# A two-layer graph kernel on one core: where the last 40 node steps scale their output, and when node types are gathered

## The chip, the cores and the metric

The kernel runs on one core of one Trainium2 chip. The metric is the device time of one execution in microseconds. Times inside an execution are microseconds from the start of its profiled span.

## What is computed

```python
# N = 50000 nodes, D = 256, E = 12500 edges (src, dst), dst sorted
# layer 0: attention over edges, 8 heads of 32
qkv = x @ W_qkv.T + b_qkv
att = einsum('mhd,mhd->mh', Q[dst], K[src]) / sqrt(32)
attention = segment_softmax(att, dst)
x = layernorm(x + segment_sum(attention * V[src], dst) @ W_ff.T + b_ff)
# layer 1: messages from node types
W = (edge_attr @ W_dist + b_dist) * cutoff(edge_weight)
agg = segment_sum(embed_table[node_type][src] * W, dst)
x = layernorm(x + concat(x, agg) @ W_comb + b_comb)
```

Most nodes receive no edge. For such a node the result needs only its own row: z = x + b_ff, a layer norm, one 256x256 product with mixed weights (`w_mix`, the identity included), and a second layer norm. The kernel computes that for all 50000 rows, and then overwrites the rows of nodes that receive edges.

## The kernel before

**Node steps.** 98 steps g = 0 to 97 of 512 rows each (the last has 336), as a tile of 128 partitions with four rows of 256 each. Four slots rotate, q = g % 4. For a step:

- SyncE loads `xin` (512 KB, L464) into its slot once the addition and the transposes of the step four before are done, and stores `on` (L473) when both halves of the output scaling have signalled (`n_od`, `n_oa`, L469 to L475). Its queue is in order: at g it issues load g+4, then store g-3, and then whatever edge or softmax traffic belongs to g.
- GpSimd adds the bias row: `zin` = `xin` + `bff_row` (`z_add`, L696). `zin` has two buffers, so the addition of g+3 waits for the statistics of g+1.
- VectorE takes statistics of `zin` (L1340) and moments (L1349), and the reciprocal `r1` (L1357) of ScalarE's root (L1053).
- TensorE transposes `xin` (L797) into two PSUM banks; ScalarE copies them to `zT` with the bias (`zT_copy`, L1046); TensorE multiplies by `w_mix` in two halves (`z_product`, L818; in steps with an edge block in three parts, L811 to L813).
- VectorE makes `yn` (`y`, L1368) in two halves h of two rows, ScalarE squares it with an accumulated sum (`squares`, L1062) and takes the root (L1067), VectorE the reciprocal `r2` (L1378).
- The output scaling `on` = `yn` * `r2`: ScalarE does rows 0 to 2 (`final`, L1075), VectorE row 3 (`final`, L1386). `split(g)` gives the number of ScalarE's rows: 3, and 2 in the last step.

**Order.** There is no scheduler: every engine runs a loop over g, and the order inside it is written out by hand. In step g VectorE does y(g-1,1), statistics g+2, y(g,0), moments g+2, r1(g+1), r2(g-1), its scaling g-1, and then the softmax piece of that step. ScalarE does root 1 (g+1), squares(g-1) with root 2, the transposed copy g+1, and its scaling g-2. TensorE does z_product(g,0), transposes g+1, z_product(g,1). GpSimd does the addition g+3, then gathers and small masks.

**Edge blocks.** Steps 9 to 57 (`LEAD` = 9, `B` = 49, `AFTER` = 58) each also handle one block of 256 edges: GpSimd gathers rows of x for receivers and sources (L705, L708, four indirect DMAs, two blocks ahead), TensorE transposes them and makes Q, K and V in three parts, VectorE takes the low parts and the scores. GpSimd also gathers the node types of the sources (`type_gather`, L699: 128 values in one indirect DMA; 98 are needed in all): one in each edge step, 25 in steps 58 to 82, and 24 more in steps 66 to 89.

**Softmax.** Steps 58 to 97 have no edge block. VectorE runs the segment softmax at the end of its steps, one piece k = g - 58 a step (`softmax_step`): comparisons (k = 0 to 3), scans over 112x896 (k = 4 with its second input in PSUM; 5, 14 and 15 with both inputs in SBUF), rows and carries through TensorE (k = 6, 8, 10, 17, 19), reciprocals (k = 21 to 24, L1536). TensorE's part waits for VectorE at the start of steps 62, 65, 67, 74 and 76 (`chunk_ends`, `carry_columns`, L898 and L904). ScalarE does the exponential at the end of step 71. In step 91 GpSimd casts the types (L761) after its addition and after all gathers have landed, and TensorE transposes them (`type_transposes`, L910) at the head of its step. In steps 85 to 92 SyncE stores the attention and loads the first edge tiles.

**Last pass.** 49 blocks again: GpSimd weighs the values (`weigh`, L715, a product of 128x512), VectorE runs the segment sums, TensorE the products, and the rows go out by indirect DMA. TensorE's first work here waits for ScalarE's `scaled(0)`, which stands behind ScalarE's last scaling.

Of the kernel before, what the change touches and what calls it, by code (L numbers as in the profile page):

```python
# [31 lines left out]
P = 128  # L32
# [14 lines left out]
def after(eng, sem, count):  # L47

    if count > 0:
        eng.wait_ge(sem, count)  # L50


def build(nc, x, src, dst, attr, weight, ntype, w_qkv, b_qkv, w_ff, b_ff, table, w_dist, b_dist, w_comb, b_comb, out):
# [35 lines left out]
    def sb(name, shape, dt=F32):  # L89
        return ctx.enter_context(nc.sbuf_tensor(name, shape, dt))  # L90
# [68 lines left out]
    sd1 = sb("sd1", [P, SLOTS, ROWS])  # L159
    r1 = sb("r1", [P, SLOTS, ROWS])  # L160
    yn = sb("yn", [P, SLOTS, ROWS * D])
    junk = sb("junk", [P, ROWS, D])
    ss = sb("ss", [P, SLOTS, ROWS])
    sd2 = sb("sd2", [P, SLOTS, ROWS])
# [234 lines left out]
    def inside(g):  # L399

        return 0 <= g < G
# [5 lines left out]
    def half(g, j):  # L407

        return 2 + (2 * g + j // 2) % 3

    def split(g):

        return 2 if g == G - 1 else 3

    def within(b):

# [214 lines left out]
    def _(pool):  # L631
# [56 lines left out]
        def z_add(g):  # L688
# [6 lines left out]
            bb = bff_row[0:np_, :].rearrange("p (a d) -> p a d", a=1).to_broadcast([np_, nj, D])  # L695
            pool.tensor_tensor(z, xx, bb, ALU.add).then_inc(n_z, 1)  # L696

        def type_gather(t):
            pool.indirect_dma_start(ty[:, t, :], None, ntype_rows, bass.IndirectOffsetOnAxis(src_i[:, t:t + 1], 0)).then_inc(n_ty, 16)  # L699

# [27 lines left out]
        for g in range(G):  # L728
            if g == LEAD - 3:
                pool.wait_ge(s_idx, 1)  # L730
                gathers(0)
            if g == LEAD - 2:
                gathers(1)
            if inside(g + 3):
                z_add(g + 3)
            b = g - LEAD
            if within(b) and within(b + 2):
                gathers(b + 2)
            if within(b):
                type_gather(b)  # L740
            if 0 <= g - AFTER < 25:
                type_gather(B + g - AFTER)
            if 8 <= g - AFTER < T - B - 17:
                type_gather(B + 17 + g - AFTER)
            if g == AFTER + 1:
                pool.wait_ge(c_mask, 1)
                pool.tensor_scalar(neg_a[:], same_c[:], FAR, -FAR, ALU.mult, ALU.add).then_inc(c_neg, 1)
            if g == AFTER + 2:
                pool.wait_ge(c_mask, 2)
                pool.tensor_scalar(neg_b[:], next_c[:], FAR, -FAR, ALU.mult, ALU.add).then_inc(c_neg, 1)  # L750
            if g == AFTER + 5:
                pool.wait_ge(c_mask, 3)
                pool.wait_ge(c_step, step["running_maximum"])
                pool.tensor_scalar(neg_a[:], first_c[:], FAR, -FAR, ALU.mult, ALU.add).then_inc(c_neg, 1)
            if g == AFTER + 6:
                pool.wait_ge(c_mask, 4)
                pool.wait_ge(c_step, step["chunk_maximum"])
                pool.tensor_scalar(neg_b[:], last_c[:], FAR, -FAR, ALU.mult, ALU.add).then_inc(c_neg, 1)
            if g == AFTER + 33:
                pool.wait_ge(n_ty, 16 * T)  # L760
                pool.tensor_copy(tyf[:], ty[:, :, 0]).then_inc(n_tf, 1)  # L761
        pool.wait_ge(c_step, step["attention"])
        pool.wait_ge(c_out, 16)
        pool.wait_ge(c_same, 16 * NCH)
# [275 lines left out]
    def _(act):  # L1040
        def zT_copy(g):
            for c in range(DC):
                act.wait_ge(n_tp, 2 * g + c + 1)
                after(act, n_y, 2 * (g - 1))
                to = z_hi if in_parts(g) else zT
                act.activation(to[:, g % 2, c, :], ps[:, c, :], ACT.Identity, bias=bff_col[:, c:c + 1]).then_inc(n_tc, 1)  # L1046
# [5 lines left out]
            after(act, n_r1, g - SLOTS + 1)  # L1052
            act.activation(sd1[0:np_, q, 0:nj], mv[0:np_, q, 0:nj, 1], ACT.Sqrt, bias=eps_col[0:np_, :]).then_inc(n_s1, 1)  # L1053

        def squares(g):
            q = g % SLOTS
            np_, nj = size(g)
            after(act, n_s2, g)
            for j in range(nj):
                if j % 2 == 0:  # L1060
                    act.wait_ge(n_yy, 2 * g + j // 2 + 1)
                last = act.activation(junk[0:np_, j, :], yn[0:np_, q, j * D:(j + 1) * D], ACT.Square,  # L1062
                                      scale=float(D ** -0.5), accum_out=ss[0:np_, q, j:j + 1])
            last.then_inc(n_ss, 1)
            act.wait_ge(n_ss, g + 1)
            after(act, n_r2, g - SLOTS + 1)
            act.activation(sd2[0:np_, q, 0:nj], ss[0:np_, q, 0:nj], ACT.Sqrt, bias=eps_col[0:np_, :]).then_inc(n_s2, 1)  # L1067

# [89 lines left out]
        for g in range(G):  # L1158
            b = g - LEAD
            if inside(g + 1):  # L1160
                std1(g + 1)
            if within(b):
                parts(b)
            if inside(g - 1):
                squares(g - 1)
            if inside(g + 1):
                zT_copy(g + 1)
            if inside(g - 2):
                final(g - 2)
            if g == 5:  # L1170
                act.wait_ge(s_echain, 7)
                act.activation(ct[:, 3, :], ct[:, 2, :], ACT.Sin, bias=half_pi[:], scale=-float(np.pi) / CUTOFF).then_inc(s_sin, 1)
            if g == 6 or g == 7:
                weight_copies(g - 6)
            if g == 3:
                act.wait_ge(s_wready, 2)
                for k in range(DC):
                    act.activation(mix_hi[:, k, :], w_mix[:, k, :], ACT.Copy).then_inc(s_mix, 1)
            if within(b):
                q_copy(b)  # L1180
                v_copy(b)
            if g == AFTER + 13:
                act.wait_ge(c_step, step["difference"])
                act.activation(ex_c[:], run_c[:], ACT.Exp, scale=SCALE).then_inc(c_ex, 1)
            if g == AFTER + 33:
                act.wait_ge(s_tyt, 1)
                act.activation(ty_rows[:], ps[0:T, A, 0:P], ACT.Copy).then_inc(s_tyc, 1)
        squares(G - 1)
        final(G - 2)
        final(G - 1)  # L1190

        act.wait_ge(c_out, 16)
# [20 lines left out]
    def _(dve):  # L1213
# [145 lines left out]
        def y(g, h):  # L1359
            q = g % SLOTS  # L1360
            np_, nj = size(g)
            dve.wait_ge(n_r1, g + 1)
            after(dve, n_ss, g - SLOTS + 1)
            after(dve, n_od, g - SLOTS + 1)
            after(dve, n_oa, g - SLOTS + 1)
            dve.wait_ge(n_y, 2 * g + h + 1)
            for j in range(2 * h, min(2 * h + 2, nj)):
                last = dve.scalar_tensor_tensor(out=yn[0:np_, q, j * D:(j + 1) * D], in0=ps[0:np_, half(g, j), (j % 2) * D:(j % 2 + 1) * D],  # L1368
                                                scalar=r1[0:np_, q, j:j + 1], in1=bc[0:np_, :], op0=ALU.mult, op1=ALU.add)
            last.then_inc(n_yy, 1)  # L1370
# [9 lines left out]
        def final(g):  # L1380
            q = g % SLOTS
            np_, nj = size(g)
            dve.wait_ge(n_r2, g + 1)
            after(dve, n_out[q], 16 * (g // SLOTS))
            for j in range(split(g), nj):
                last = dve.tensor_scalar(on[0:np_, q, j * D:(j + 1) * D], yn[0:np_, q, j * D:(j + 1) * D],  # L1386
                                         r2[0:np_, q, j:j + 1], None, ALU.mult)
            last.then_inc(n_od, 1)

        def receiver_low(n):  # L1390
# [223 lines left out]
        rstd1(0)  # L1614
        for g in range(G):
            b = g - LEAD
            if inside(g - 1):
                y(g - 1, 1)
            if inside(g + 2):
                stats(g + 2)  # L1620
            if within(b):
                receiver_low(b)
            y(g, 0)
            if within(b):
                source_low(b)
            if inside(g + 2):
                moments(g + 2)
            if inside(g + 1):
                rstd1(g + 1)
            if inside(g - 1):  # L1630
                rstd2(g - 1)
            if in_parts(g + 1):
                z_low(g + 1)
            if within(b):
                scores(b)
            if inside(g - 1):
                final(g - 1)
            if g == 4:
                edge_floats()
            if g == 5:  # L1640
                edge_cutoffs()
            if g == 6:
                edge_indices()
            if g == 6 or g == 7:
                weight_low(g - 6)
            if g == 7:
                bias_parts()
            if g == 4:
                dve.wait_ge(s_mix, 2)
                for k in range(DC):  # L1650
                    dve.tensor_tensor(mix_lo[:, k, :], w_mix[:, k, :], mix_hi[:, k, :], ALU.subtract).then_inc(s_mix, 1)
            if g == LEAD + 30:
                table_parts()
            softmax_step(g - AFTER)
        y(G - 1, 1)
        rstd2(G - 1)
        final(G - 1)

        dve.wait_ge(c_out, 16)
        dve.wait_ge(c_same, 16 * NCH)  # L1660
# [38 lines left out]
```

## Time and profile before

| | us |
|---|---|
| median of 3 runs | 1166.85 (1166.7 to 1167.99) |
| the profiled execution's own time | 1165.22 |
| its span | 1163.5 |
| TensorE busy, share of the span | 1072.6, 92% |
| VectorE | 987.6, 85% |
| ScalarE | 799.1, 69% |
| GpSimd | 694.1, 60% |

The profile is of one execution. Busy time is the union of an engine's instructions; on GpSimd the issue of an indirect DMA counts as an instruction. PE is TensorE's multiplication, PEld its weight load, DVE VectorE, ACT ScalarE, POOL GpSimd, SPq SyncE's queue. "[0.55 <-ACT zT L1046]" behind a row says that the engine was idle for 0.55 us before it, and what ended that. PEclk is the granted TensorE clock as a share of 2.4 GHz.

### The profile page before, as it was taken

How to read it: one execution, taken by the hardware profiler on the slowest of the kernel's cores; microseconds unless marked ns; L12 is line 12 of the kernel's file. 1: busy time of each engine (PE TensorE's matmuls, PEld its weight loads, DVE VectorE, ACT ScalarE, POOL GpSimd, SP SyncE). 2: the span in 40 equal slices, each digit the busy share in tenths (PEclk: the TensorE clock that was granted, in tenths of full speed). 3: DMA queues.
4: the chain of work that ended last, by engine and by line, in shares of the span. 5: the costliest groups of instructions: out<-in, count | busy, mean ns of one | idle time of the engine just before them, and what ended most of it. 6: DMA issues, size and time to landing. Idle time of an engine off the chain costs nothing.

```text
span 1163.5 us, 24929 instructions
## 1 busy us (share of the span) xinstructions
PE 1072.6 (92%) x7106; PEld 987.7 (85%) x7106; DVE 987.6 (85%) x2646; ACT 799.1 (69%) x2464; POOL 694.1 (60%) x558
## 2 busy tenths in 40 slices
PE   4959999999999999999887878879999999999994
PEld 3759999999999999999666767668888888888883
DVE  4978888888888888887989899868888888888882
ACT  2857777777777777777778878884555555555553
POOL 4367777777777777775777776413444444444442
PEclk9979999999999999999989999989999999999997
DMA  4856666666666666665545556646666666666740
GB/s 147 274 210 211 229 226 225 229 232 221 220 219 218 218 228 229 224 224 179 199 148 179 181 183 224 235 154 168 174 171 177 182 183 185 187 185 180 185 139 33
DMA packets 121385, 227.23 MB, mean 195 GB/s; under 512 B 33587, under 2 KB 61486, under 8 KB 121184
## 3 DMA queue, kind: packets, MB, share of 16 engines
q1 hardware_dynamic: 104000, 189.54, 49.0%
q0 software_dynamic: 17248, 36.08, 11.4%
q8 instruction: 59, 0.97, 0.4%
q14 instruction: 78, 0.64, 0.2%
HBM read 137.84 MB, written 93.59 MB: 199 GB/s over the span
## 4 chain that ended last, share of the span: by engine, by line
PE 78%; DVE 8%; issue 6%; ACT 3%; DMA 2%; POOL 1%; SPq 1%; DVEq 0%; POOLq 0%; ACTq 0%
PE ps L938 14%; PE ps L920 7%; PE ps L818 5%; PE ps L797 5%; PE ps L812 4%; PE ps L811 4%; PE ps L856 4%; PE ps L855 4%; PE ps L857 4%; PE ps L813 4%; PE ps L969 4%; PE ps L853 2%; DVE stat L1340 2%; DVE yn L1368 2%; PE ps L962 2%
## 5 line engine op out<-in xcount | busy, mean ns | idle before, releaser
L696 POOL TENSOR_TENSOR zin<-xin,bff_row 128x1024 f32<-128x1024 f32 x98 | 233.4, 2384 | 78.6 <-DVE stat L1340 62.7
L818 PE MATMUL ps<-w_mix,zT 128*128 128x256 f32 x780 | 193.5, 396 | 33.8 <-ACT zT L1046 32.7
L818 PEld LDWEIGHTS ps<-w_mix,zT 128*128 128x128 f32 x780 | 146.2, 196 | 62.9 <-ACT zT L1046 41.8
L1368 DVE SCALAR_TENSOR_TENSOR yn<-ps,r,bc 128x256 f32<-128x256 f32 x391 | 169.2, 473 | 28.6 <-PE ps L813 15.3
L1062 ACT ACTIVATE junk<-yn 128x256 f32<-128x256 f32 x391 | 158.1, 416 | 45.6 <-DVE yn L1368 45.3
L715 POOL TENSOR_TENSOR ev<-abc,v 128x512 f32<-128x512 f32 x49 | 66.2, 1353 | 198.1 <-DVE zeT L1560 198.1
L1340 DVE BATCH_NORM_STATS2 stat<-zin 128x6 f32<-128x256 f32 x391 | 136.2, 409 | 9.4 <-POOL zin L696 9.4
L705 POOL DMA_INDIRECT xd<-in_x_dram,idx x98 | 94.2, 961 | 78.3 <-PE ps L841 47.0
L1075 ACT ACTIVATE on<-yn,r 128x256 f32<-128x256 f32 x293 | 126.7, 501 | 0.0
L721 POOL DMA_INDIRECT out_dram<-oe,idx x98 | 98.1, 1001 | 33.8 <-issue 22.1
L811 PE MATMUL ps<-mix_hi,z_hi 128*128 128x256 f32 x392 | 114.8, 293 | 2.6 <-DVE z_lo L1405 2.6
L699 POOL DMA_INDIRECT ty<-in_node_type_dram,src_i x98 | 101.9, 1040 | 24.5 <-issue 20.9
L1386 DVE TENSOR_SCALAR on<-yn,r 128x256 f32<-128x256 f32 x98 | 110.4, 1126 | 1.7
L708 POOL DMA_INDIRECT xs<-in_x_dram,idx x98 | 93.6, 955 | 29.9 <-issue 29.6
L812 PE MATMUL ps<-mix_lo,z_hi 128*128 128x256 f32 x392 | 110.8, 283 | 0.0
L813 PE MATMUL ps<-mix_hi,z_lo 128*128 128x256 f32 x392 | 110.0, 281 | 0.0
L797 PE MATMUL ps<-ident,xin 128*128 128x128 f32 (+1 forms) x782 | 105.9, 280 | 0.0
L797 PEld LDWEIGHTS ps<-ident,xin 128*128 128x128 f32 (+1 forms) x782 | 94.4, 146 | 6.2 <-issue 1.4
L938 PE MATMUL ps<-wc,agg 128*128 128x256 f32 x392 | 98.4, 379 | 0.0
L920 PE MATMUL ps<-num,wff 128*128 128x256 f32 x392 | 93.4, 381 | 0.0
L938 PE MATMUL ps<-w_mix,zeT 128*128 128x256 f32 x392 | 92.6, 379 | 0.0
L1153 ACT ACTIVATE oe<-ye,er 128x256 f32<-128x256 f32 x98 | 44.5, 501 | 61.5 <-DVE er L1609 61.5
(202 smaller groups left out, 3079.4 us busy)
## 6 DMA issues: line engine op xcount, KB each, us to landing
xin<-in_x_dram SPq DMA_DIRECT2D x97, 512.0 KB, 4.7
out_dram<-on SPq DMA_DIRECT2D x97, 512.0 KB, 2.9
xd_o<-xdT SPq DMA_DIRECT2D x49, 256.0 KB
v_o<-vT SPq DMA_DIRECT2D x49, 256.0 KB, 2.0
v<-v_o SPq DMA_DIRECT2D x49, 256.0 KB
abc<-a_o SPq DMA_DIRECT2D x196, 64.0 KB
xd<-xd_o SPq DMA_DIRECT2D x49, 256.0 KB, 4.3
sbc<-same_o SPq DMA_DIRECT2D x49, 128.0 KB, 4.0
```

What stands on the lines that cost most here:

```text
L696: pool.tensor_tensor(z, xx, bb, ALU.add).then_inc(n_z, 1)
L797: last = pe.transpose(ps[:, c, j * P:j * P + np_], xin[0:np_, q, j * D + c * P:j * D + (c + 1) * P], ident[0:np_, 0:np_])
L811: mm(to, hi, mix_hi[:, k, :], start=k == 0, stop=False)
L812: mm(to, hi, mix_lo[:, k, :], start=False, stop=False)
L813: last = mm(to, lo, mix_hi[:, k, :], start=False, stop=k == DC - 1)
L818: last = mm(ps[0:np_, half(g, j), (j % 2) * D:(j % 2 + 1) * D], zT[:, g % 2, k, j * P:j * P + np_], w_mix[:, k, :], start=k == 0, stop=k = ...
L920: last = mm(bank(FF[par])[:, c, :], wff[:, k, c * P:(c + 1) * P], num[:, par, k, :], start=k == 0, stop=k == DC - 1)
L938: last = mm(to[:, t, :], cols_of[:, k, t * P:(t + 1) * P], weights[:, k, :], start=k == 0 and not bias, stop=k == DC - 1)
L1062: last = act.activation(junk[0:np_, j, :], yn[0:np_, q, j * D:(j + 1) * D], ACT.Square, scale=float(D ** -0.5), accum_out=ss[0:np_, q, j:j ...
L1075: last = act.activation(on[0:np_, q, j * D:(j + 1) * D], yn[0:np_, q, j * D:(j + 1) * D], ACT.Copy, scale=r2[0:np_, q, j:j + 1])
L1340: last = dve.bn_stats(stat[0:np_, g % SLOTS, j, :], zin[0:np_, g % 2, j * D:(j + 1) * D])
L1368: last = dve.scalar_tensor_tensor(out=yn[0:np_, q, j * D:(j + 1) * D], in0=ps[0:np_, half(g, j), (j % 2) * D:(j % 2 + 1) * D], scalar=r1[0 ...
```

## The change

`relaxed(g)` is true from step 58 on. Four things differ.

1. **Scaling.** From step 57 on `split` is 2: ScalarE scales rows 0 and 1 of each step, and a new GpSimd `final` scales rows 2 and 3 in one instruction of 128x512, with `r2` repeated along each row. VectorE scales nothing there.
2. **ScalarE's order** in steps 58 to 97: squares of the first half of g-1, scaling g-2, transposed copy g+1, squares of the second half, root 2. `squares` is cut in two, each half with its own wait and signal, so that waits on `n_ss` count two a step. VectorE takes `r2(g-2)` at the head of step g and not `r2(g-1)` behind r1.
3. **Type gathers.** Two in each of the 49 edge steps, none later.
4. **VectorE's scaling** in steps up to 56 also writes the sum of each row to a new tile `row_sum`, which nothing reads.

```diff
+    def relaxed(g):
+        return g >= AFTER
     def split(g):
-        return 2 if g == G - 1 else 3
+        return 2 if relaxed(g + 1) else 3
...
+        def final(g):
+            q = g % SLOTS
+            np_, nj = size(g)
+            n = nj - split(g)
+            pool.wait_ge(n_r2, g + 1)
+            after(pool, n_out[q], 16 * (g // SLOTS))
+            rows = [a[0:np_, q, split(g) * D:nj * D].rearrange("p (j d) -> p j d", j=n) for a in (on, yn)]
+            scale = r2[0:np_, q, split(g):nj].rearrange("p (j a) -> p j a", a=1).to_broadcast([np_, n, D])
+            pool.tensor_tensor(rows[0], rows[1], scale, ALU.mult).then_inc(n_od, 1)
...
             if within(b):
-                type_gather(b)
-            if 0 <= g - AFTER < 25:
-                type_gather(B + g - AFTER)
-            if 8 <= g - AFTER < T - B - 17:
-                type_gather(B + 17 + g - AFTER)
+                type_gather(2 * b)
+                type_gather(2 * b + 1)
+            if relaxed(g - 1):
+                final(g - 2)
...
+        final(G - 2)
+        final(G - 1)
...
-        def squares(g):
+        def squares(g, h):
             after(act, n_s2, g)
-            for j in range(nj):
-                if j % 2 == 0:
-                    act.wait_ge(n_yy, 2 * g + j // 2 + 1)
+            act.wait_ge(n_yy, 2 * g + h + 1)
+            for j in range(2 * h, min(2 * h + 2, nj)):
                 last = act.activation(junk[0:np_, j, :], ...)
             last.then_inc(n_ss, 1)
-            act.wait_ge(n_ss, g + 1)
+        def std2(g):
+            act.wait_ge(n_ss, 2 * (g + 1))
...
             if inside(g - 1):
-                squares(g - 1)
-            if inside(g + 1):
-                zT_copy(g + 1)
-            if inside(g - 2):
+                squares(g - 1, 0)
+            if relaxed(g):
                 final(g - 2)
+                if inside(g + 1):
+                    zT_copy(g + 1)
+                squares(g - 1, 1)
+                std2(g - 1)
+            else:
+                if inside(g - 1):
+                    squares(g - 1, 1)
+                    std2(g - 1)
+                if inside(g + 1):
+                    zT_copy(g + 1)
+                if inside(g - 2):
+                    final(g - 2)
...
-        squares(G - 1)
+        squares(G - 1, 0)
         final(G - 2)
+        squares(G - 1, 1)
+        std2(G - 1)
         final(G - 1)
...
             for j in range(split(g), nj):
                 last = dve.tensor_scalar(on[0:np_, q, j * D:(j + 1) * D], yn[0:np_, q, j * D:(j + 1) * D],
-                                         r2[0:np_, q, j:j + 1], None, ALU.mult)
+                                         r2[0:np_, q, j:j + 1], None, ALU.mult, ALU.add, accum_out=row_sum[0:np_, q, j:j + 1])
...
+            if relaxed(g - 1):
+                rstd2(g - 2)
             if inside(g - 1):
                 y(g - 1, 1)
...
-            if inside(g - 1):
+            if inside(g - 1) and not relaxed(g):
                 rstd2(g - 1)
...
-            if inside(g - 1):
+            if inside(g - 1) and not relaxed(g):
                 final(g - 1)
...
+        rstd2(G - 2)
         y(G - 1, 1)
         rstd2(G - 1)
-        final(G - 1)
```

## Rows read from the trace of the kernel before

**Rows 1.** Windows by stage.

```profile
core 0: us, PE busy (x) PEld busy (x) DVE busy (x) ACT busy (x) POOL busy (x), PEclk, DMA share, GB/s
...
87.00:542.00 455.00, 453.89 (x3847) 450.68 (x3845) 395.85 (x1019) 349.84 (x1005) 340.26 (x284) 1.00 0.67 223
...
551.00:773.00 222.00, 186.41 (x959) 155.88 (x958) 205.39 (x614) 179.23 (x584) 145.24 (x91) 0.96 0.54 185
...
727.00:738.00 11.00, 9.87 (x52) 7.95 (x50) 10.93 (x30) 8.76 (x30) 5.69 (x3) 1.00 0.94 304
```

**Rows 2.** Timeline of a plain step: start us, length us, engine.

```profile
711.17 1.39 DVE L1340 BATCH_NORM_STATS2 stat<-zin 128x6 f32<-128x256 f32 x4
...
712.42 1.25 ACT L1046 ACTIVATE zT<-ps,bff_col 128x512 f32<-128x512 f32 x2
...
712.70 2.37 POOL L696 TENSOR_TENSOR zin<-xin,bff_row 128x1024 f32<-128x1024 f32 x1 [1.28 <-DVE stat L1340]
...
713.72 1.59 PEld L818 LDWEIGHTS ps<-w_mix,zT 128*128 128x128 f32 x8 [0.55 <-ACT zT L1046]
...
713.78 1.44 DVE L1386 TENSOR_SCALAR on<-yn,r 128x256 f32<-128x256 f32 x1
...
715.14 0.86 DVE L1368 SCALAR_TENSOR_TENSOR yn<-ps,r,bc 128x256 f32<-128x256 f32 x2
...
715.34 1.01 PEld L797 LDWEIGHTS ps<-ident,xin 128*128 128x128 f32 x8
...
716.32 1.60 PEld L818 LDWEIGHTS ps<-w_mix,zT 128*128 128x128 f32 x8
...
717.18 1.25 ACT L1046 ACTIVATE zT<-ps,bff_col 128x512 f32<-128x512 f32 x2
```

**Rows 3.** Line groups: VectorE's scaling, 551 to 725 us; ScalarE's scaling, squares.

```profile
L1386 DVE TENSOR_SCALAR on<-yn,r x30: 353/1433/1448, 552.1 to 723.3; 128x256 f32<-128x256 f32 x30
...
L1075 ACT ACTIVATE on<-yn,r 128x256 f32<-128x256 f32 x293 | 126.7, 501 | 0.0
...
L1062 ACT ACTIVATE junk<-yn 128x256 f32<-128x256 f32 x391 | 158.1, 416 | 45.6 <-DVE yn L1368 45.3
```

**Rows 4.** Timeline: transposed copies of the last two steps.

```profile
765.22 1.25 ACT L1046 ACTIVATE zT<-ps,bff_col 128x512 f32<-128x512 f32 x2
...
769.67 1.25 ACT L1046 ACTIVATE zT<-ps,bff_col 128x512 f32<-128x512 f32 x2
```

**Rows 5.** Line groups: GpSimd's type gathers, 97 to 540 us; its L715.

```profile
L699 POOL DMA_INDIRECT ty<-in_node_type_dram,src_i x48: 947/952/966, 100.0 to 534.9; - x48
...
L715 POOL TENSOR_TENSOR ev<-abc,v 128x512 f32<-128x512 f32 x49 | 66.2, 1353 | 198.1 <-DVE zeT L1560 198.1
```

**Rows 6.** Timeline: two scans on VectorE, gathers beside them.

```profile
576.10 2.01 DVE L1489 TENSOR_TENSOR_SCAN run_c<-neg_a,ps 112x896 f32<-112x896 f32 x1
576.16 0.97 POOL L699 DMA_INDIRECT ty<-in_node_type_dram,src_i  x1
...
582.77 2.01 DVE L1493 TENSOR_TENSOR_SCAN seg_c<-neg_b,run_c 112x896 f32<-112x896 f32 x1
582.84 2.75 POOL L699 DMA_INDIRECT ty<-in_node_type_dram,src_i  x1 [0.15 <-issue]
```

**Rows 7.** Timeline: ScalarE's transposed copies around a reciprocal step.

```profile
689.66 1.25 ACT L1046 ACTIVATE zT<-ps,bff_col 128x512 f32<-128x512 f32 x2
...
695.79 1.25 ACT L1046 ACTIVATE zT<-ps,bff_col 128x512 f32<-128x512 f32 x2
```

**Rows 8.** Timeline: TensorE's weight loads, start of step 67.

```profile
602.43 0.46 PEld L904 LDWEIGHTS ps<-one_col,cr 1*112 1x112 f32 x4 [3.33 <-DVE cr L1460]
602.91 3.02 PEld L818 LDWEIGHTS ps<-w_mix,zT 128*128 128x128 f32 x8
```

**Rows 9.** Timeline: the type transposes of step 91.

```profile
739.35 2.35 POOL L696 TENSOR_TENSOR zin<-xin,bff_row 128x1024 f32<-128x1024 f32 x1 [3.46 <-DMA xin<-in_x_dram]
...
742.03 0.32 PE L910 MATMUL ps<-ident,tyf 128*98 128x128 f32 x1 [3.87 <-POOL tyf L761]
```

More of the change, by code:

```diff
@@ L161, in build @@
     yn = sb("yn", [P, SLOTS, ROWS * D])
+    row_sum = sb("row_sum", [P, SLOTS, ROWS])
     junk = sb("junk", [P, ROWS, D])
@@ L1064, in squares @@
             last.then_inc(n_ss, 1)
-            act.wait_ge(n_ss, g + 1)
+        def std2(g):
+            q = g % SLOTS
+            np_, nj = size(g)
+            act.wait_ge(n_ss, 2 * (g + 1))
             after(act, n_r2, g - SLOTS + 1)
@@ L1362, in y @@
             dve.wait_ge(n_r1, g + 1)
-            after(dve, n_ss, g - SLOTS + 1)
+            after(dve, n_ss, 2 * (g - SLOTS + 1))
             after(dve, n_od, g - SLOTS + 1)
```

## The prediction

> **What bounds the kernel now.** I read the busy shares and the stages first, then the timeline of one plain step, then what ends each wait. In the 49 steps with an edge block TensorE is busy 453.9 of 455 us, so nothing else counts there; the last 40 node steps take 222 us, or 5.55 us a step, with TensorE at 186 us, ScalarE at 179 us and VectorE at 205 us [rows 1]. A plain step of this stretch (no softmax work) shows why. From one transposed copy on ScalarE to the next are 717.18 - 712.42 = 4.76 us. VectorE starts its output scaling at 713.78 and its next instruction at 715.14, 0.07 us after GpSimd's addition (712.70 + 2.37) ended; TensorE waited 0.55 us for a transposed copy [rows 2]. The scaling has a median of 1433 ns but a shortest of 353 ns [rows 3]: some 1.1 us of it is waiting until GpSimd is through. So VectorE bounds the plain step, and a fifth to a quarter of its step is a wait for the other engine. Softmax steps are longer, as their extra instruction comes behind it.
>
> **The other floors.** TensorE: 8 + 8 + 8 weight loads start at 713.72, 715.34 and 716.32, the last lot runs 1.60 us, so 4.2 us a step [rows 2]. ScalarE: at the very end VectorE waits for others, and copy to copy is 769.67 - 765.22 = 4.45 us [rows 4]; one output row less, 501 ns by its record [rows 3] and some 0.4 of the engine's time where records overlap, makes 4.0 to 4.05. VectorE without the scaling: 4.76 - 1.36 = 3.4 us. GpSimd: 2.37 us of addition, and the new scaling of 128x512 with two inputs. The nearest row is the product at L715, 1.35 us [rows 5]; bounds are 1.2 us (half of the 1024-wide addition) and, if the repeated scalar operand costs double, 2.7 us. I take 1.35, the same shape and engine: 2.37 + 1.35 + 0.25 of gaps = 4.0 us. The plain step should so become 4.25 us, TensorE's.
>
> **What the shared path of GpSimd and VectorE does.** Two neighbours in the trace separate it. A 2.01 us scan whose second input is in PSUM runs beside a type gather of 0.97 us; a scan of the same 2.01 us with both inputs in SBUF stretches the gather that starts 0.07 us behind it to 2.75 us [rows 6]. So GpSimd and a two-input VectorE instruction exclude each other, and the VectorE scaling (one input) is excluded too when it comes second [rows 2, 3]. No row shows a two-input VectorE instruction coming second, since the scaling has always taken up the wait ahead of it. Its cost is bounded by nothing and by the 1.36 us the scaling now waits; I take 1.36, as the scaling behaves so. The Trainium skill, SBUF — State Buffer, "Who interferes with whom", says that a VectorE instruction with two SBUF inputs contends with a GpSimd one that reads SBUF, and that whichever starts first blocks the other fully; by it the sum is the one below, without it that of the first rival.
>
> **The sum, part by part** (profiled execution, 1165.2 us; the median of the three is 1166.85, 1.6 above).
> 1. Scaling leaves VectorE, steps 58 to 97. GpSimd's addition still starts right behind the statistics, so whatever VectorE issues after its reciprocals still meets it.
>  - Six steps end in softmax work with one SBUF input or none shared (62: scan on PSUM, 70, and 79 to 82, four reciprocals, in steps of 695.79 - 689.66 = 6.13 us [rows 7]). Each gains 1.36 less 0.08 for the reciprocal now at the head: 7.7 us.
>  - Six plain steps (71, 84 to 87, 92) go from 4.76 to 4.25: 3.0 us.
>  - Steps 88 and 89 took 11 us together, with 304 GB/s and DMA at 0.94 [rows 1], because the rows of x and so the addition came late and the scaling waited for it; 93 is like them. The scaling's wait is gone, and the statistics that need the addition come a step later: 3.4 us.
>  - In 64, 66 and 75 copies out of PSUM run ahead of the blocked instruction: 1.6 us.
>  - Thirteen steps (58 to 61, 63, 65, 68, 69, 72, 73, 77, 78, 83) end in an instruction with two inputs or a fast copy or scalar form. It waits for the addition in the scaling's place. Gain nothing; the reciprocal at the head costs 0.08 each: -1.0 us.
> 2. ScalarE's order. In plain steps both orders fit under 4.25. Where TensorE has waited for VectorE (602.43, waited 3.33 us [rows 8]; likewise in 74 and 76), the step is a chain: products, transposes, copy, and now two squares and the root behind the copy before VectorE's next step may start. Two squares more, 0.42 each with some 0.1 of reading the accumulator [rows 3], less one output row (0.4): -0.5 each, -1.5 us. Scaling on ScalarE now stands ahead of the copy and waits for the reciprocal at the head of VectorE's step; in a 6 us step this delays TensorE inside its slack, at nothing. Without that slack it would cost what VectorE is late by, up to 1.4 us a step.
> 3. Clock. After the wait at 602.43 eight loads took 3.02 us and not 1.60 [rows 8], and the granted clock shows the lower level there. The like wait ahead of step 76 was a little shorter and grows by about half a us, so I charge half of such a stretch (half of 1.4 to 1.7): -0.8 us.
> 4. The type transposes in step 91. TensorE waited 3.87 us for GpSimd's cast, which stood behind an addition whose rows were 3.46 us late [rows 9]. Now 1.35 us of scaling stands between addition and cast, and at a faster pace the rows are later against the step: I take 2 us, between none and 5. -3.4 us.
> 5. End. Step 94 was VectorE catching up and now costs TensorE's 4.25; the last squares stand behind the copy: -1.0 us. The last GpSimd scaling and the first L715 product (1.35 each) lie beside ScalarE's last rows and the first edge matmuls.
> 6. Type gathers, edge stage. GpSimd is idle 455 - 340.3 = 114.7 us there, 2.34 a block [rows 1]; one more gather is 0.95 us plus 0.3 of issue [rows 5], hidden by that idle time, and no row gather, addition or SP queue entry behind it is needed sooner than a block later. Its 128 tiny transfers add little to DMA. Nothing in, nothing out: 0. In the tail, its removal frees GpSimd for the scaling. If the cover were gone each would cost 1.25.
> 7. The accumulating scaling, steps 0 to 56. It should no longer wait for GpSimd, nor be as short as 0.35; hidden by TensorE in the edge stage. In steps 0 to 8 it may give or take 1 us: 0.
> 8. SP: a store now waits for GpSimd too, whose scaling of a step ends over two steps before the load behind that store is wanted: 0, or 1 us a step should GpSimd fall behind.
>
> Gains 15.7, costs 7.7: net 8.0 us, 1157.2 in the profiled execution, **1158.5** at the median. Own range: 1154 to 1163.
>
> **Rivals.** A measurement tells 0.2% (2.3 us) from no change.
> - **No blocking when VectorE is second.** Then the thirteen steps gain too: 13 x 1.15, less 1 for the score transposes in 59: 14 us more, **1145**. For it: no row shows such a block. Against: the stretched gather [rows 6] and the scaling [rows 3]. 18%.
> - **The tail gives it back.** The rows of x come 5 us late for the type handshake and not 2, and three more waits of TensorE bring the low clock at 1.5 to 1.7 us each: 8 us, **1166**. For: both have happened once [rows 8, 9]. Against: less waiting elsewhere keeps TensorE busier. 10%.
> - **GpSimd becomes the bound (slower).** Place: its scaling in each of 40 steps. If the repeated scalar makes it 2.7 us, its step is 5.3 us; 14 plain steps (71, 84 to 96) lose 0.95 each and the rest about 1: +14, **1173**. It decides from about 2.3 us. Against: L715 [rows 5]. For: no row has this operand form. 7%.
> - **The second gather stretches in the edge stage.** If it took 2.75 us [rows 6] with 0.3 of issue, 0.7 us a block would stick out: 49 x 0.7 = 35, **1193**. It decides when more than 2.34 us is added a block. Against: 48 of 48 gathers there take 947 to 966 ns. 5%.
> - My forecast: 60%.
>
> **Numbers.** Faster by over 0.2% (below 1164.5): 60 + 18 + 2 of the second rival = 80%; within it 8%; slower 7 + 5 = 12%. The range takes in the first rival and my own bounds and stops short of the slower ones: 1145 to 1165.
>
> **What would show it.** Right: plain steps at 4.2 to 4.3 us with no VectorE scaling; reciprocal steps near 4.8; in step 63 the scan starts when the addition ends, and its step is no shorter than before; the edge stage still saturated by TensorE; scaling there near 0.5 us; GpSimd's scaling 1.3 to 1.4 us; TensorE waiting 5 us or more for the cast in step 91. Wrong: softmax steps shorter by 1.3 us (first rival), a plain step above 4.5, GpSimd busy nine tenths and more of the tail, or a longer edge stage.

## The result and the profile after

The changed kernel takes 1178.06 us, median of seven runs, against 1166.77 for the kernel before in the same session: a ratio of 1.0097, 95% interval 1.0077 to 1.0116. The prediction was 1158.5 us with a range of 1145 to 1165. The profiled execution took 1179.73 us (span 1178.0), and its trace is compared here with that of before. Windows by stage of the changed kernel:

```profile
core 0: us, PE busy (x) PEld busy (x) DVE busy (x) ACT busy (x) POOL busy (x), PEclk, DMA share, GB/s
87.00:560.00 473.00, 449.91 (x3764) 440.71 (x3764) 388.59 (x1041) 343.25 (x987) 392.01 (x327) 1.00 0.62 210
578.00:786.00 208.00, 187.71 (x959) 160.01 (x959) 174.37 (x576) 165.94 (x550) 128.41 (x80) 0.93 0.61 200
```

Beside [rows 1] two things stand out. TensorE, which had been busy 453.9 of 455 us in the edge-block steps, is now idle 23 of 473 us there. And GpSimd, taken as busy, has gone from 340 to 392 us. The last 40 steps are shorter. Measured from the first VectorE instruction of a step's y to that of another step (by this measure "the edge stage" is steps 9 to 57 and "the last steps" are 58 to 96, in all that follows):

```
                        before    after
steps 0 to 8             60.77    59.06
steps 9 to 57           463.90   492.23   (edge blocks: 9.44 -> 10.10 us each from step 13 on)
steps 58 to 96          222.33   208.08
```

So the gain that the forecast was about is there, and larger (14.3 us). A loss of 28.3 us stands in a stage for which the forecast said 0.

**What GpSimd does in an edge block.** Timelines of GpSimd, before (a block from 328.50 on) and after (from 303.67 on), start and length in us:

```profile
328.50 2.40 POOL L696 TENSOR_TENSOR zin<-xin,bff_row 128x1024 f32<-128x1024 f32 x1
331.93 0.96 POOL L705 DMA_INDIRECT xd<-in_x_dram,idx  x1 [1.02 <-PE ps L841]
333.19 0.96 POOL L705 DMA_INDIRECT xd<-in_x_dram,idx  x1 [0.30 <-issue]
...
336.97 0.95 POOL L699 DMA_INDIRECT ty<-in_node_type_dram,src_i  x1 [0.30 <-issue]
337.94 2.41 POOL L696 TENSOR_TENSOR zin<-xin,bff_row 128x1024 f32<-128x1024 f32 x1
```

```profile
303.67 2.41 POOL L701 TENSOR_TENSOR zin<-xin,bff_row 128x1024 f32<-128x1024 f32 x1
306.24 1.24 POOL L720 DMA_INDIRECT xd<-in_x_dram,idx  x1 [0.16 <-issue]
307.78 0.95 POOL L720 DMA_INDIRECT xd<-in_x_dram,idx  x1 [0.30 <-issue]
...
311.55 0.95 POOL L714 DMA_INDIRECT ty<-in_node_type_dram,src_i  x1 [0.30 <-issue]
312.81 0.95 POOL L714 DMA_INDIRECT ty<-in_node_type_dram,src_i  x1 [0.30 <-issue]
313.76 2.41 POOL L701 TENSOR_TENSOR zin<-xin,bff_row 128x1024 f32<-128x1024 f32 x1
```

Before, GpSimd waited once in a block for another engine, 1.02 us ahead of the first xd gather (for TensorE's transposes, which free the buffer). Nearly all its other idle time is the 0.30 us "issue" between gathers, which is part of what a gather costs: it stays when nothing else is waited for, as the block after shows. After, it waits for nobody: 313.76 - 303.67 = 10.09 us of its own work, one instruction behind the other, is the block.

**How the other engines are held.** In the changed kernel z_add has slid until it lies on VectorE's xd_lo. First VectorE's row in the same block, then all xd_lo of the kernel (shortest, median, longest in ns), then the group of weight loads at the head of q_product, 124 to 559 us:

```profile
305.29 1.34 DVE L1425 TENSOR_TENSOR xd_lo<-xdT,xd_hi 128x512 fp32r<-128x512 f32 x1
```

```profile
L1425 DVE TENSOR_TENSOR xd_lo<-xdT,xd_hi x49: 670/1342/1493, 84.6 to 568.2; 128x512 fp32r<-128x512 f32 x49
```

```profile
L869 PEld LDWEIGHTS ps<-b_rows,ones_r 128*128 128x128 f32 x172 | 32.3, 188 | 31.3 <-issue 31.3
```

z_add ends at 303.67 + 2.41 = 306.08. xd_lo (two inputs in SBUF) starts at 305.29 and ends 0.55 us after that, so it stood still for most of the 0.79 us that z_add had left: a median of 1342 ns, and 674 before. q_product needs xd_lo, so TensorE stands idle ahead of its loads at L869, 31.3 us over 43 blocks (before, 4.1 us over 44). The profile puts that down to "issue", though what is late is xd_lo; only the order of starts shows it (xd_lo ends at 306.63, the first of these matmuls starts at 306.73). The xd gather that starts beside xd_lo takes 1.24 us, where the others take 0.95.

**The last 40 steps.** The timeline of the scan of step 63 with z_add beside it and of TensorE's weight loads at the type transposes of step 91, then all of GpSimd's and VectorE's scaling:

```profile
604.99 2.37 POOL L701 TENSOR_TENSOR zin<-xin,bff_row 128x1024 f32<-128x1024 f32 x1
...
605.89 3.35 DVE L1524 TENSOR_TENSOR_SCAN seg_c<-neg_b,run_c 112x896 f32<-112x896 f32 x1
...
755.51 0.16 PEld L926 LDWEIGHTS ps<-ident,tyf 128*98 128x98 f32 x1 [5.13 <-POOL tyf L775]
755.58 3.08 PEld L834 LDWEIGHTS ps<-w_mix,zT 128*128 128x128 f32 x8
```

```profile
L711 POOL TENSOR_TENSOR on<-yn,r x41: 682/1040/1050, 581.3 to 789.8; 128x512 f32<-128x512 f32 x40, 112x256 f32<-112x256 f32 x1
...
L1417 DVE TENSOR_SCALAR_CACHE_REDUCE on<-yn,r x57: 469/470/482, 31.0 to 574.2; 128x256 f32<-128x256 f32 x57
```

The scan takes 3.35 us and not 2.01 [rows 6]: it is held until z_add ends (607.36) and ends 1.88 us after that. So a two-input instruction is held when it comes second, as forecast, and the first rival is out. GpSimd's scaling takes 1.04 us. The accumulating scaling takes 0.47 us in all 57 cases. In step 91 TensorE's loads wait 5.13 us for the cast, where they waited 4.27 before, and its next eight loads take 3.08 us, where they took 2.28 before and take 1.60 at the full clock.

### The profile page after: what moved, and what is told of

Read it like the earlier page. It is cut to its first block, busy times and chain, and to the rows that moved or that the text cites. A ratio compares the mean times of both kernels' runs of the same rounds, so it can differ in the third digit from the quotient of the medians.

```text
span 1178.0 us, 25043 instructions
## 1 busy us (share of the span) xinstructions
PE 1080.1 (92%) x7106; PEld 992.1 (84%) x7106; DVE 955.5 (81%) x2662; ACT 784.6 (67%) x2424; POOL 739.4 (63%) x599
## 4 chain that ended last, share of the span: by engine, by line
PE 81%; issue 7%; DVE 5%; ACT 3%; POOL 2%; DMA 1%; DVEq 0%; SPq 0%; POOLq 0%; ACTq 0%
PE ps L954 14%; PE ps L834 8%; PE ps L936 7%; PE ps L813 5%; PE ps L872 4%; PE ps L827 4%; PE ps L871 4%; PE ps L873 4%; PE ps L829 4%; PE ps L828 4%; PE ps L985 4%; PE ps L869 3%; PE ps L978 2%; PE ps L893 2%; PE ps L894 2%
## 5 line engine op out<-in xcount | busy, mean ns | idle before, releaser
L834 PEld LDWEIGHTS ps<-w_mix,zT 128*128 128x128 f32 x780 | 148.9, 199 | 42.5 <-ACT zT L1062 19.5
L720 POOL DMA_INDIRECT xd<-in_x_dram,idx x98 | 106.4, 1086 | 35.0 <-issue 22.3
L1094 ACT ACTIVATE on<-yn,r 128x256 f32<-128x256 f32 (+1 forms) x253 | 111.0, 500 | 16.3 <-DVE r L1409 16.3
L827 PE MATMUL ps<-mix_hi,z_hi 128*128 128x256 f32 x392 | 114.7, 293 | 2.7 <-DVE z_lo L1436 2.7
L723 POOL DMA_INDIRECT xs<-in_x_dram,idx x98 | 93.7, 956 | 29.9 <-issue 29.6
L714 POOL DMA_INDIRECT ty<-in_node_type_dram,src_i x98 | 93.7, 956 | 29.6 <-issue 29.6
L1126 ACT ACTIVATE vT<-ps,bqkv 128x256 f32<-128x256 f32 x98 | 41.1, 471 | 92.3 <-PE ps L895 92.3
```

Of the source, the lines that this page charges most:

```text
L827: mm(to, hi, mix_hi[:, k, :], start=k == 0, stop=False)
L834: last = mm(ps[0:np_, half(g, j), (j % 2) * D:(j % 2 + 1) * D], zT[:, g % 2, k, j * P:j * P + np_], w_mix[:, k, :], start=k == 0, stop=k = ...
L1094: last = act.activation(on[0:np_, q, j * D:(j + 1) * D], yn[0:np_, q, j * D:(j + 1) * D], ACT.Copy, scale=r2[0:np_, q, j:j + 1])
```

## The experiments

Slack is what an engine could take on in a block without making the block longer. Theory G: the loss is the second gather, which is more than GpSimd's real slack of some 1.03 us a block. Theory S: it reaches TensorE through z_add holding up xd_lo. Rivals: some other part of the change lengthens the blocks, or the last steps' gain comes from the gathers having left them. Ratios are to the kernel before, with 95% intervals; stage times are taken as in the table above.

**The gathers alone.** In the kernel before:

```
-                type_gather(b)
-            if 0 <= g - AFTER < 25: ...
-            if 8 <= g - AFTER < T - B - 17: ...
+                type_gather(2 * b)
+                type_gather(2 * b + 1)
```

> The kernel before with one edit: both type gathers in each edge-block step and none in the last 40 steps. Theory G (the second gather fills GpSimd): GpSimd has 1.03 us of real slack in a block and the gather takes 0.95 and 0.30 to issue, so blocks go from 9.44 to about 10.1 us from the third or fourth block on, +25 to +30 us in the edge stage; the last 40 steps as before or up to 2 us shorter (gathers gone), type transposes +3 as they wait for the cast: 1190 to 1197 in all. Rival V (the accumulating scaling or another part of the change slows the blocks): blocks stay at 9.44 and the time within 3 us of the kernel before.

Measured: 1186.64 us, 1.0182 (1.0148 to 1.0215). Steps 9 to 57 take 485.13 us, +21.2, blocks 9.88 us: theory G, though less than the 10.1 and the 25 to 30 us expected. The last steps take 220.7 (-1.6); steps 90 and 91 with the type transposes are 2.7 us shorter (9.81 for 12.55), where 3 us more were expected. Here it is the scaling that is held (all of it, shortest, median and longest in ns; then one in a block's timeline):

```profile
L1383 DVE TENSOR_SCALAR on<-yn,r x98: 344/1664/2545, 30.5 to 795.4; 128x256 f32<-128x256 f32 x97, 112x256 f32<-112x256 f32 x1
```

```profile
310.00 2.15 DVE L1383 TENSOR_SCALAR on<-yn,r 128x256 f32<-128x256 f32 x1
```

xd_lo keeps 0.67 us and no gather is stretched. A block's GpSimd work is then 9.83 to 9.9 us: 2.40, six gathers at 0.95 and their gaps. By the order of starts, VectorE, held up by the scaling, is what passes that on here.

**The change without its gathers.** The edit is the reverse, made in the changed kernel.

> The changed kernel with its type gathers as in the kernel before: one per block, the other 49 in the last 40 steps. Theory G: blocks at 9.44 us again, the last 40 steps keep 10 to 14 us of their gain: 1152 to 1157. Rival V: blocks stay near 10.1 us, time 1175 or more. Rival P (the gathers in the last 40 steps were what held those back, so moving them made the gain there): blocks 9.44, last steps as before, time 1163 to 1167.

Measured: 1159.38 us, 0.9940 (0.9915 to 0.9965). Blocks are back at 9.44 us (462.7 in the stage), so nothing else lengthens them. But the last steps gain only 4 us (218.35). GpSimd's timeline there has no gap either:

```profile
657.54 1.05 POOL L711 TENSOR_TENSOR on<-yn,r 128x512 f32<-128x512 f32 x1
658.54 2.38 POOL L701 TENSOR_TENSOR zin<-xin,bff_row 128x1024 f32<-128x1024 f32 x1
661.08 1.86 POOL L714 DMA_INDIRECT ty<-in_node_type_dram,src_i  x1 [0.16 <-issue]
663.24 0.95 POOL L714 DMA_INDIRECT ty<-in_node_type_dram,src_i  x1 [0.31 <-issue]
664.21 1.05 POOL L711 TENSOR_TENSOR on<-yn,r 128x512 f32<-128x512 f32 x1
```

In a step with two gathers the scaling on GpSimd does not fit beside them: steps 79 to 83 take 29.6 us, 24.3 in the changed kernel. That is half of the 10.3 us lost against the changed kernel. Another 3.4 stand in steps 90 and 91 (19.32 for 15.94): TensorE waits 8.55 us there for the cast. This expectation (10 to 14 us kept) was wrong.

**The accumulating scaling alone.** In the kernel before, `accum_out=row_sum[...]` added to VectorE's scaling (the sums are not used).

> The kernel before with the row sum added to VectorE's scaling everywhere and nothing else. Theory A (a form that never waits for GpSimd is a large part of what the last 40 steps gained): the scaling falls from 1.07 to 0.47 us (0.08 more for reading the sum), plain steps from 4.76 to about 4.5, 4 to 8 us less in all: 1159 to 1163. Rival O (the order of ScalarE is the bound there, and the gain needs it): scaling 0.47, plain steps still 4.7 or more, time within 2 us of before. Blocks at 9.44 in both.

Measured: 1152.95 us, 0.9884 (0.9852 to 0.9916): 14 us for one operand, where 4 to 8 were expected. The last steps take 210.55 us, -11.8 where the whole change has -14.3; blocks stay at 9.44. Why is in two rows, GpSimd's and VectorE's:

```profile
700.00 2.36 POOL L697 TENSOR_TENSOR zin<-xin,bff_row 128x1024 f32<-128x1024 f32 x1 [0.33 <-DVE stat L1341]
...
701.08 0.48 DVE L1387 TENSOR_SCALAR_CACHE_REDUCE on<-yn,r 128x256 f32<-128x256 f32 x1
```

The scaling starts and ends while z_add runs, where the plain form took 1.44 us [rows 2].

**xd_lo from PSUM.** In the changed kernel, same values, same waits:

```
-            dve.tensor_tensor(xd_lo[:], xdT[:, n % 2], xd_hi[:], ALU.subtract)
+            dve.tensor_tensor(xd_lo[:], bank(A), xd_hi[:], ALU.subtract)
```

> The changed kernel, with xd_lo's subtraction reading the transposes in PSUM and not their copy in SBUF, so that it has one SBUF input. Same values, same waits, same GpSimd work. Theory S (the coupling to the other engines goes through z_add holding up xd_lo): xd_lo back to about 0.68 us, blocks 9.44 to 9.5 for most of the stage, 20 to 28 us less than the changed kernel: 1150 to 1158. Theory G alone (GpSimd's own work is the bound whatever waits for it): blocks at 9.75 to 10.1 us, which is the sum of z_add 2.40, six gathers at 0.95 and six gaps at 0.30 or a little over, 0 to 13 us less: 1165 to 1178.

Measured: 1158.39 us, 0.9924 (0.9902 to 0.9946), with 473.4 us in steps 9 to 57. That is 19.7 us less than the changed kernel, at the edge of what theory S said (20 to 28). Both theories hold, one after the other: blocks stay at 9.44 us up to step 35 and take 9.83 in steps 36 to 38 and from step 43 on. Windows of an early and a late stretch, then all xd_lo, then a late block of GpSimd:

```profile
160.00:340.00 180.00, 179.59 (x1522) 178.07 (x1521) 145.72 (x422) 138.81 (x399) 149.28 (x128) 1.00 0.68 222
430.00:545.00 115.00, 112.35 (x936) 109.59 (x935) 91.43 (x263) 85.53 (x249) 94.69 (x84) 1.00 0.64 214
```

```profile
L1425 DVE TENSOR_TENSOR xd_lo<-ps,xd_hi x49: 667/673/680, 84.7 to 549.4; 128x512 fp32r<-128x512 f32 x49
```

```profile
505.22 2.39 POOL L701 TENSOR_TENSOR zin<-xin,bff_row 128x1024 f32<-128x1024 f32 x1
507.78 0.97 POOL L720 DMA_INDIRECT xd<-in_x_dram,idx  x1 [0.16 <-issue]
...
515.05 2.40 POOL L701 TENSOR_TENSOR zin<-xin,bff_row 128x1024 f32<-128x1024 f32 x1
```

GpSimd's own work is 515.05 - 505.22 = 9.83 us a block, 0.39 more than TensorE's 9.44. For some 26 blocks, 10 us in sum, it falls behind at no cost; then it is the bound. With xd_lo in SBUF the block is 10.10 from the fifth on (step 13), for z_add holds xd_lo, which stretches the gather behind z_add (1.24 us there, 0.97 here), which makes GpSimd later still.

**Gathers and accumulating scaling together,** both edits in the kernel before.

> The kernel before with both edits together that were tried alone: two gathers in each block and the accumulating scaling; old order, one row of scaling on VectorE. Alone, the gathers gave blocks of 9.88 us with the scaling held to 2.1 us and xd_lo at 0.67. Theory S2 (the form that no longer waits for GpSimd lets VectorE reach xd_lo while z_add runs, so xd_lo is held and stretches the gather behind z_add): blocks at 10.10 us, xd_lo at about 1.34, first xd gather 1.24, edge stage 491 to 493 and not 485; the last 40 steps about 209: 1180 to 1184. Rival (the rest of the changed kernel is what takes the blocks from 9.88 to 10.10): blocks at 9.83 to 9.88, edge stage 483 to 485, 1172 to 1176.

Measured: 1185.30 us, 1.0145 (1.0111 to 1.0179); steps 9 to 57 take 492.00 us (with the gathers alone 485.13), blocks 10.10:

```profile
304.35 1.34 DVE L1392 TENSOR_TENSOR xd_lo<-xdT,xd_hi 128x512 fp32r<-128x512 f32 x1
...
305.30 1.24 POOL L706 DMA_INDIRECT xd<-in_x_dram,idx  x1 [0.16 <-issue]
```

These are the changed kernel's blocks to 0.02 us. The form that did not wait for GpSimd costs 6.9 us in the edge stage: the scaling that waited used to keep VectorE behind z_add, and now xd_lo meets it. In the last steps it gives back 6.4 (214.33 for 220.72), and not the 11.8 that it gave without the moved gathers: the steps that it shortens are shorter here too, but steps 90 and 91 are 5.1 us longer (14.87 for 9.81). TensorE's loads there wait 4.5 us for the cast, 3.3 with the gathers alone; the cast stands behind an addition of GpSimd that waits 2.2 us for rows of x. The 209 us expected for the last steps were wrong, and the total came out 1.3 above the range.

**The cast early.** In the changed kernel the cast of the types is moved from step 91 to step 78 (`if g == AFTER + 33` becomes `AFTER + 20`).

> The changed kernel with the cast of the gathered types at step 78 and not in step 91, where it stands behind a z_add that waits for its input rows. Theory Q (the cast's place in GpSimd's queue is what holds TensorE up there): TensorE's 4.7 us wait and the low clock after it are gone, steps 90 and 91 fall from 15.94 to about 12 us, 3 to 5 us less than the changed kernel: 1173 to 1175. Rival D (the input rows are late in that stretch whatever is done, and TensorE would wait for them a little later): steps 90 and 91 shorter, steps 92 to 96 longer by the same, time within 1.5 us of the changed kernel.

Measured: 1171.33 us, 1.0041 (1.0024 to 1.0058), 6.7 less than the changed kernel's median and more than the 3 to 5 expected. Steps 90 and 91 take 8.77 us and not 15.94, as two plain steps, and steps 92 to 96 are no longer than they were. Rival D is out. TensorE's matmuls there, without a wait:

```profile
749.19 0.27 PE L926 MATMUL ps<-ident,tyf 128*98 128x128 f32 x1
749.30 1.89 PE L834 MATMUL ps<-w_mix,zT 128*128 128x256 f32 x8
```

**The order without GpSimd's scaling.** In the kernel with gathers as before, the accumulating scaling and the new order of ScalarE and VectorE, with the one row's scaling left on VectorE (three on ScalarE).

> The kernel before with the accumulating scaling and the new order of ScalarE and VectorE in the last 40 steps, but with one row's scaling left on VectorE and three on ScalarE; type gathers as before. The kernel with the accumulating scaling alone took 1152.95 us, its last steps 210.55. Theory A (the form of the scaling is the gain, the order adds little): within 3 us of 1153, plain steps 84 to 89 at 3.8 to 4.46 us as there. Rival O (the order gives a step that was bound by ScalarE's chain another 0.3 to 0.5 us): 1140 to 1148. If the order costs (as at steps 74 and 76 of the changed kernel, where the copies find the clock low): 1155 to 1158.

Measured: 1152.65 us, 0.9877 (0.9842 to 0.9911), last steps 211.1. The order alone gives nothing that can be told from the accumulating scaling alone. The change without its gathers, which differs from this kernel only in having two rows of scaling on GpSimd in place of one on VectorE and one more on ScalarE, is 6.7 us slower; in the last steps 7.3, of which 4.6 stand in steps 90 and 91 (19.32 and 14.74), so much of it is a later cast.

**A candidate.** The changed kernel with three edits: xd_lo from PSUM, the cast at step 78, and the gathers where GpSimd has time. The edit of the gathers (`types` counts up from 0):

```
-                type_gather(2 * b)
-                type_gather(2 * b + 1)
+                type_gather(next(types))
+                if b % 8 != 4:
+                    type_gather(next(types))
+            if g == LEAD - 1:
+                for _ in range(3):
+                    type_gather(next(types))
+            if g in (AFTER + 5, AFTER + 14, AFTER + 15):
+                type_gather(next(types))
```

> A candidate: the changed kernel with xd_lo reading PSUM, the cast at step 78, and the gathers spread by GpSimd's real slack: 3 in step 8 (idle 4.35 us there), two in each block but six, which have one, and 3 in the last 40 steps. GpSimd's work over the 49 blocks is 49 times 9.83 less 6 times 1.25, or 474.2 us against 463 for the blocks; the slack that was used up in 27 blocks of 0.39 with xd_lo on PSUM was about 10.5 us. By that blocks stay at 9.44 but for the last few: edge stage 462 to 464, last 40 steps 203 to 206: 1142 to 1147. If the head's three gathers only shift the start, or DMA holds the last steps: 1148 to 1153.

Measured: 1145.54 us, 0.9815 (0.9787 to 0.9842), faster than both kernels and within the 1142 to 1147 expected. Windows of its two stages:

```profile
85.00:551.00 466.00, 464.49 (x3919) 460.08 (x3918) 376.59 (x1088) 357.70 (x1028) 383.57 (x328) 1.00 0.67 221
551.00:751.00 200.00, 182.26 (x956) 155.85 (x955) 175.23 (x575) 165.16 (x548) 132.66 (x83) 0.96 0.65 208
```

TensorE is saturated again, with 43 more gathers hidden; four blocks at the end take 9.6 to 9.8 us and the one in step 56 10.57 (before 9.45), 2.2 us in sum, so by my estimate about two gathers too many are left there.

**The candidate less one part.** First with the old order and without GpSimd's scaling; then with the new order, still without GpSimd's scaling; then with xd_lo read from SBUF.

> The kernel with the gathers spread (1145.54 us), without its new order and without GpSimd's scaling: the kernel before with the accumulating scaling, xd_lo from PSUM, the spread gathers and the cast at step 78. It parts the gain of the last 40 steps. Theory A (the form of the scaling is most of it): plain steps 79 to 82 at 5.18 and not 4.67, steps 84 to 89 at 3.8 to 4.46 and not 3.56 to 4.33, the last 40 steps at 203 to 206 us and not 200.85: 1147 to 1151. Rival M (order and GpSimd's scaling are as large a part): 1153 to 1158.

> As the spread kernel (1145.54 us), with the new order of ScalarE and VectorE, but one row's scaling left on VectorE and three on ScalarE, none on GpSimd. It parts order from GpSimd's scaling. If the order is the part that pays: within 2 us of the spread kernel. If it is GpSimd's scaling that pays, since it takes 0.5 us of ScalarE's work out of a step that ScalarE bounds: as without both, or 1 to 2 us worse (steps 79 to 82 at 5.07): 1148 to 1153.

> As the spread kernel (1145.54 us), with xd_lo reading the copy in SBUF again. Theory S2 (xd_lo with two SBUF inputs is what couples GpSimd's lateness to TensorE before its queue is truly late): the 43 blocks with two gathers go to about 10.10 us once z_add has drifted onto xd_lo, three or four blocks in, the six with one gather pull it back by 0.6 to 0.9 us each: edge stage 482 to 488 us and not 465.3: 1162 to 1168. Rival (with the work of GpSimd cut to its slack the form of xd_lo does not matter): edge stage 463 to 468, 1144 to 1149.

Measured: 1151.66 us, 0.9874 (0.9833 to 0.9916); 1153.94, 0.9894 (0.9854 to 0.9934); 1163.60, 0.9983 (0.9966 to 1.0000). The last steps of the first two take 207.7 and 207.3 us, the candidate's 200.85: the new order is worth nothing that shows, GpSimd's scaling 6.5 us once its queue is nearly free of gathers. The first came out above the range for theory A (1147 to 1151; 203 to 206 in the last steps), below the rival's: the form of the scaling is most of the gain, and GpSimd's scaling is more of it than I thought. Without xd_lo from PSUM the edge stage is back at 483.3 us, as expected, blocks at 10.10 us but for those around the six with one gather:

```profile
L1432 DVE TENSOR_TENSOR xd_lo<-xdT,xd_hi x49: 670/1341/1494, 84.7 to 559.3; 128x512 fp32r<-128x512 f32 x49
```

## Why the prediction was wrong

**The step that failed is part 6 of the sum,** "GpSimd is idle 455 - 340.3 = 114.7 us there, 2.34 a block [...] hidden by that idle time". Idle by the busy count is not free. In the block shown above, four issue gaps of 0.30 us and at least 0.16 behind z_add belong to GpSimd's own instructions. What is left is the wait of 1.02 less 0.16, or 0.86 us. I charged the new gather its 0.30 of issue and left out that the four others have theirs. 1.25 - 0.86 = 0.39 us a block sticks out, as the late blocks with xd_lo from PSUM show (9.83 against 9.44). With the loop through xd_lo it is 0.66. The fourth rival named this place, but with the same slack, so it decided at "more than 2.34 us" and looked for a stretch of the type gather. That stayed away (median 0.95 us, the longest of 93 at 1.24); the gather stretched was xd's.

**Part 7 (accumulating scaling, 0)** was right for it alone in the edge stage (463.05 us for 463.90) and wrong in company: it lets VectorE run onto z_add at xd_lo, 6.9 us. The rule that a two-input instruction waits when it comes second was used in the forecast for the last steps, and not asked of the edge stage, where the phase of the two engines was about to move.

**The last steps** came out at -14.3 us against -8.0. By groups (sums of steps, from the two traces):

```
                                            forecast   measured
six softmax steps (62, 70, 79 to 82)           -7.7       -8.8
six plain steps (71, 84 to 87, 92)             -3.0       -4.6
steps 88, 89, 93                               -3.4       -3.8
steps 64, 66, 75                               -1.6       +0.1
thirteen steps with a held instruction         +1.0       -2.7
order and low clock (67, 74, 76)               +2.3       +2.4
steps 90 and 91                                +3.4       +3.4
steps 94 to 96                                 +1.0       -0.3
```

Most of the mechanisms stand, but some sizes were off, and some of the agreement is luck. TensorE's floor was read too low. With no wait its loads run in turns of 4.33 us and not 4.2:

```profile
760.48 3.32 PEld L834 LDWEIGHTS ps<-w_mix,zT 128*128 128x128 f32 x16
763.83 1.01 PEld L813 LDWEIGHTS ps<-ident,xin 128*128 128x128 f32 x8
```

The next product starts at 764.81, 4.33 after the first. Steps 88 and 89 take these 4.33. The plain steps that are shorter (71 and 84 at 3.56, 85 and 86 at 4.12 and 4.06) are VectorE catching up behind a long step, and with that the group gained more than forecast. The other rows:

- The row that was furthest off is the thirteen steps with a held instruction: most of them gained some 0.1 to 0.4 us each in place of losing 0.08. In step 63 the scan, 2.01 us long, ends 1.88 behind z_add, so 0.13 of it was done by then; before, it ended 2.09 behind z_add, as the scaling stood between them.
- Single steps from 64 to 77 can't be read to better than 2 us: the changed kernel with the early cast has the same instructions there, and its step 73 takes 8.63 us and not 6.62. So the agreement of the row for order and low clock is not told from chance.
- That of steps 90 and 91 is luck in part. TensorE's wait was to grow by 3.35 us and grew by 0.86 (4.27 to 5.13). The low clock behind it, of which that part of the sum says nothing, took another 0.8 on eight loads. From TensorE's transposes of step 91 to those of step 93 are 16.0 us, and 14.5 before: 1.5 more and not 3.4.
- GpSimd's scaling took 1.04 us where I took 1.35 from a product in the last pass; nothing hung on that.
- Two slips of the sums change nothing: 1157.2 and 1.6 are 1158.8, and a GpSimd step of 5.3 us is 1.05 above the plain step and not 0.95.

What the forecast missed is that most of the gain did not need the move: the accumulating form alone brings 11.8 us in the last steps. The Trainium skill, SBUF — State Buffer, "Who interferes with whom", names tensor_scalar among the operations that can take the pair of ports shared with GpSimd, and leaves out the form that also writes its accumulator; the trace agrees (0.48 us inside z_add, where the plain form took 1.44). The forecast used that only for the steps where the edit was made, and did not ask whether the same form would do in the last steps, in place of the move.

**The first rival** (a two-input instruction is not held) is refuted by the 3.35 us scan and by xd_lo. **The second** (the tail gives it back) and **the third** (GpSimd bound by its scaling) did not happen. A sign of the second did: the granted clock in the last steps fell from 0.96 [rows 1] to 0.93, and yet they were shorter. The third's place was the wrong one, for GpSimd did become the bound, in the edge stage.

## What to carry to other kernels

Slack of an engine is what it waits for others in a step, read from the timeline of one step; gaps that belong to its own instructions are work. Before work is moved onto an engine, set its whole sequence against the step of the bound, and ask what its instructions will lie on once it runs later. And before work is moved off an engine because it is blocked, try a form that is not: one added operand gave 11.8 us in the last steps, where the whole change gave 14.3.

## What was not expected

- The same instruction pays or costs by its phase. The accumulating scaling: -11.8 us in the last steps alone, +6.9 in the edge stage beside a second gather. GpSimd's scaling: +6.7 us with gathers in its queue (1152.65 to 1159.38), -8.4 with nearly none (1153.94 to 1145.54), medians in both. Of the 8.4, 6.5 stand in the last steps; some 3 lie behind them, in the last pass, and stay unexplained.
- With xd_lo from PSUM, an engine that is late by 0.39 us a block costs nothing for 26 blocks and then all of it. That kernel, tried on half the blocks, would by this have shown no loss. Where another engine is held up meanwhile, as in the changed kernel, the loss starts with the fifth block.
- A gather on GpSimd is stretched by VectorE instructions with two SBUF inputs: 0.95 us alone, 1.24 beside xd_lo, 1.86 beside the one of a softmax step.
- Eight weight loads behind a wait of 5.13 us took 3.08 us and not 1.60, at a granted clock of 0.50. With the wait gone, both went: 7.2 us in two steps. How long that wait is differs by kernel: 4.27 us before, 5.3 with the accumulating scaling alone, 8.55 with the change without its gathers.
